# Linear-attention and FFN block on one core: another path and another order for the first chunk

## The reference

```python
xn = layernorm(x)                       # x: (8, 1024, 256), fp32
q, k, v = xn @ Wq.T, xn @ Wk.T, xn @ Wv.T          # 16 heads of 16
q, k = elu(q) + 1, elu(k) + 1
kv_state = sum over tokens of k (outer) v ; k_state = sum over tokens of k
attn = (q @ kv_state) / max(q . k_state, 1e-6)
local = conv over tokens, 3 taps per channel, of xn, + conv_b
attn_part = (attn + local) @ Wp.T + bp
ffn_part  = (silu(xn @ Wg.T) * (xn @ Wu.T)) @ Wd.T  # int weights / 127, hidden 768
out = x + attn_part + ffn_part
```

## Time and profile before

| | us |
|---|---|
| three runs, median | 522.21 (521.63 to 524.03) |
| the profiled execution | 524.11 |
| its span (first to last instruction) | 522.5 |
| PE busy | 499.1 (96%) |
| DVE busy | 436.5 (84%) |
| ACT busy | 332.8 (64%) |
| POOL busy | 129.7 (25%) |
| `project_kv(0)` of chunk (0, 1) starts | 48.10 |

### The profile page before, as it was taken

How to read it: one execution, slowest core, us unless ns; L and a number is a source line. 1 busy time by engine, 2 the same in 40 slices (tenths; PEclk the granted TensorE clock), 3 DMA queues, 4 the chain that set the end, 5 groups by cost and what they waited for, 6 DMA issues and landing times.

```text
span 522.5 us, 11639 instructions
## 1 busy us (share of the span) xinstructions
PE 499.1 (96%) x4249; PEld 303.9 (58%) x4249; DVE 436.5 (84%) x868; ACT 332.8 (64%) x521; POOL 129.7 (25%) x146
## 2 busy tenths in 40 slices
PE   7878999999999999999999999999999999999876
PEld 7435455665647566564756556475655647565465
DVE  4989798878888898888888888888888888886784
ACT  1576767667485766748576674857667485766730
POOL 3151414140321414032141403114140411400020
...
GB/s 231 274 57 111 87 69 94 42 130 39 157 41 110 94 41 127 42 153 40 113 88 41 126 44 150 40 115 86 40 129 43 149 40 120 43 54 31 1 41 80
DMA packets 70718, 45.90 MB, mean 88 GB/s; under 512 B 35488, under 2 KB 70176, under 8 KB 70688
## 3 DMA queue, kind: packets, MB, share of 16 engines
...
...
## 4 chain that ended last, share of the span: by engine, by line
PE 71%; DVE 11%; issue 7%; ACT 6%; DMA 2%; POOL 1%; SPq 1%; DVEq 0%; ACTq 0%
PE ps L970 16%; PE ps L1124 15%; PE ps L1054 15%; PE ps L1105 10%; PE ps L1114 10%; PE ps L1008 5%; ACT q_neg L477 3%; DVE hid L840 3%; DVE y L751 3%; DVE q_sb L809 2%; DMA wd_int<-in_L_ffn_w_down_dram 1%; DMA x_in<-in_L_attn_x_dram 1%; ACT act_g L486 1%; DVE hl L846 1%; DVE bn_raw L543 1%
## 5 line engine op out<-in xcount | busy, mean ns | idle before, releaser
L486 ACT ACTIVATE act_g<-ps,scales 128x512 f32<-128x512 f32 x96 | 65.9, 687 | 46.4 <-PE ps L1114 44.9
L840 DVE SCALAR_TENSOR_TENSOR hid<-act_g,scales,ps 128x512 f32<-128x512 f32 x96 | 71.4, 744 | 27.7 <-ACT act_g L486 27.6
L846 DVE TENSOR_TENSOR hl<-hid,hh 128x512 f16<-128x512 f32 x96 | 65.9, 687 | 1.5
L345 POOL TENSOR_TENSOR xT<-xh,xl 128x1024 f32<-128x1024 f16 x16 | 33.9, 2121 | 123.9 <-DMA xl<-xn_l 111.2
L1105 PE MATMUL ps<-xh,g_wh 128*128 128x512 f16 x192 | 57.6, 381 | 6.5 <-DVE hid L840 6.1
L494 ACT ACTIVATE hh<-hid 128x512 f16<-128x512 f32 x96 | 59.7, 622 | 5.3 <-DVE hid L840 5.3
L453 ACT ACTIVATE k_neg<-ps,scales 128x512 f32<-128x512 f32 x32 | 22.0, 687 | 57.7 <-PE ps L1054 57.7
L1114 PE MATMUL ps<-xl,u_wh 128*128 128x512 f16 x192 | 57.1, 379 | 0.0
L1114 PE MATMUL ps<-xl,g_wh 128*128 128x512 f16 x192 | 57.1, 379 | 0.0
L1105 PE MATMUL ps<-xh,u_wh 128*128 128x512 f16 x192 | 57.1, 379 | 0.0
L427 ACT ACTIVATE local<-xT,cb,cw 128x512 f32<-128x512 f32 x32 | 24.4, 806 | 42.7 <-POOL xT L345 39.3
...
## 6 DMA issues: line engine op xcount, KB each, us to landing
...
wg_int<-in_L_ffn_w_gate_dram SPq DMA_DIRECT2D x1, 768.0 KB, 7.3
wu_int<-in_L_ffn_w_up_dram SPq DMA_DIRECT2D x1, 768.0 KB, 8.8
wd_int<-in_L_ffn_w_down_dram SPq DMA_DIRECT2D x1, 768.0 KB, 6.0
wk_raw<-in_L_attn_Wk_dram ACTq DMA_DIRECT2D x1, 256.0 KB, 4.7
```

The source lines that it names most:

```text
L486: nc.scalar.activation(act_g[:, j % 2, :], ps[:, gate_bank(j), :], ACT.Silu, scale=silu_in).then_inc(silu_ready, 1)
L840: nc.vector.scalar_tensor_tensor(out=hid[:, j % 2, :], in0=act_g[:, j % 2, :], scalar=h_mul, in1=ps[:, gate_bank(j) + 1, :], op0=ALU.mult, ...
L846: nc.vector.tensor_tensor(hl[:, j, :], hid[:, j % 2, :], hh[:, j, :], ALU.subtract).then_inc(hl_ready, 1)
```

## The change

Only chunk (0, 0) is worked in another way; all later chunks keep their instructions, save that `x_high` and `x_low` of chunk (0, 1)'s step stand one j earlier (`FIRST_X_SPLIT` 2 for 3).

- x's first chunk is loaded in two halves, one from SP's queue and one from ACT's ahead of Wk and Wv. The second chunk of x comes right behind Wg and Wu, Wd comes ahead of Wp, and the bias last. The first chunk's two DMA transposes go.
- DVE normalises tiles 0 and 1, POOL tiles 2 and 3. PE transposes the eight 128x128 blocks of fp32 `xn` (`turn_first`), ACT copies them to `xT`, then makes `xh` from it, and POOL the rest `xl`.
- Keys and values are 16 fp32 matmuls of raw weights and `xT` (`project_first`), no split weights are needed for them; the scales of `key_parts` change to match. The split key and value weights are made later, for chunk (0, 1).
- POOL adds `k_sb`. `u_wh` moves from ACT to DVE.
- q is projected into banks 4 and 5 behind the keys and values, and read (`query_parts`, `relu_q`, `put_q`) after the FFN of the chunk.
- The maxima make four groups for three, and they pass PE between the new matmuls; `accumulate` goes behind `gate_up(0)`. The last group's scales and `attention_scales` come after `put_res`.
- PE's warm-up is 18 matmuls in one piece, for 24 and 16.

The core of the diff:

```diff
-        GROUPS = [["k", "v", "q"], ["g", "u"], ["d", "cw", "cb", "p"]]
+        GROUPS = [["k", "v", "q"], ["g", "u"], ["d"], ["cw", "cb", "p"]]
...
                      lambda channels: channels[:, c, :, :, :])
-            sp.dma_start(x_in[:, 0, :, :], x_v[0]).then_inc(x_loaded[0], 16)
+            sp.dma_start(x_in[:, 0, 0:2, :], x_v[0][:, 0:2, :]).then_inc(first_x[0], 16)
             load_weights("q", wqT, w_raw["q"][:, :, :])
             load_weights("g", wgT, ffn_rows("g", wgT))
             load_weights("u", wuT, ffn_rows("u", wuT))
-            sp.dma_start(bp_sb[:, :], bp.rearrange("(o n) -> o n", o=1).broadcast_to([P, D])).then_inc(bias_in, 16)
-            turn_x(0, 0)
+            sp.dma_start(x_in[:, 1, :, :], x_v[1]).then_inc(x_loaded[1], 16)
+            load_weights("d", wdT, ffn_rows("d", wdT))
             load_weights("p", wpT, w_raw["p"][:, :, :])
-            load_weights("d", wdT, ffn_rows("d", wdT))
             sp.dma_start(cw_raw[:, :, :], conv_w.rearrange("(k p) t -> p k t", p=P)).then_inc(small_in, 16)
             sp.dma_start(cb_raw[:, :], conv_b.rearrange("(k p) -> p k", p=P),
                          allow_slow_non_contiguous=True).then_inc(small_in, 16)
-            sp.dma_start(x_in[:, 1, :, :], x_v[1]).then_inc(x_loaded[1], 16)
+            sp.dma_start(bp_sb[:, :], bp.rearrange("(o n) -> o n", o=1).broadcast_to([P, D])).then_inc(bias_in, 16)
...
             nc.gpsimd.tensor_tensor(rstd[:, 0, :], var_eps[:, 0, :], half[:, :], ALU.pow).then_inc(rstd_ready, 1)
             pool.wait_ge(rstd_ready, 1)
-            normalise(0, 0)
-            normalise(0, 1).then_inc(xn_ready, 1)
-            normalise(0, 2)
+            normalise(0, 2).then_inc(xn_ready, 1)
             normalise(0, 3).then_inc(xn_ready, 1)
-            put_xT(0, 0)
-            add_x(0, 0)
+            pool.wait_ge(first_xh, 1)
+            nc.gpsimd.tensor_tensor(xl[:, 0, :, :, :], xT[:, 0, :, 1:1 + CHUNK].rearrange("p k (i t) -> p i k t", i=TILES),
+                                    xh[:, 0, :, :, :], ALU.subtract).then_inc(first_xl, 1)
+            for p in range(2):
+                pool.wait_ge(k_parts, p + 1)
+                nc.gpsimd.tensor_tensor(k_sb[:, 2 * p:2 * p + 2, :], k_exp[:, p, :, :], k_relu[:, p, :, :],
+                                        ALU.add).then_inc(k_ready, 1)
             def step(b, c, attend, ahead):
                 if ahead:
                     nb, ncx = (b, 1) if c == 0 else (b + 1, 0)
                     layernorm(nb, ncx)
+                    if isinstance(b, int) and b == 0 and c == 0:
+                        for p in range(2):
+                            pool.wait_ge(xn_h_ready, p + 1)
+                            tiles = slice(2 * p, 2 * p + 2)
+                            nc.gpsimd.tensor_tensor(xn_l[:, tiles, :], xn[:, tiles, :], xn_h[:, tiles, :],
+                                                    ALU.subtract).then_inc(xn_l_ready, 1)
+                        add_x(0, 0)
                     add_x(nb, ncx)
-                if ahead:
                     put_xT(nb, ncx)
...
+                        act.wait_ge(xh_turned, at(b, c, 16, -16))
...
-            x_high(0, 0)
-            high(kv_w[0][:, :, 0:D], w_raw["k"][:, :, :], "k", k_hi)
-            high(q_w[0][:, :, :], w_raw["q"][:, :, :], "q", q_hi)
+            for p in range(2):
+                act.wait_ge(first_turned, p + 1)
+                nc.scalar.activation(xT[:, 0, :, 1 + p * PAIR:1 + (p + 1) * PAIR], halves(FIRST_TURNED[p]),
+                                     ACT.Copy).then_inc(first_xT, 1)
+            act.wait_ge(first_xT, 2)
+            nc.scalar.activation(xh[:, 0, :, :, :], xT[:, 0, :, 1:1 + CHUNK].rearrange("p k (i t) -> p i k t", i=TILES),
+                                 ACT.Copy).then_inc(first_xh, 1)
             def middle_tap(b, c, k):
...
                     nc.scalar.activation(k_neg[:, p, :, :], ps[:, bank:bank + 2, 0:D], ACT.Relu,
-                                         scale=k_flip).then_inc(k_flipped, 1)
+                                         scale=k_flip if past else -1.0 / X_UP).then_inc(k_flipped, 1)
                     nc.scalar.activation(k_relu[:, p, :, :], ps[:, bank:bank + 2, 0:D], ACT.Relu,
-                                         scale=k_down)
+                                         scale=k_down if past else 1.0 / X_UP)
+                    if not past and p == 0:
+                        high(q_w[0][:, :, :], w_raw["q"][:, :, :], "q", q_hi)
...
-                if not past:
-                    high(u_w[0][:, :, :], ffn_raw["u"][:, :].rearrange("p (k n) -> p k n", k=KT), "u", gate_up_hi)
-                query_parts()
+                if past:
+                    query_parts()
+                else:
...
+                        high(kv_w[0][:, :, D:2 * D], w_raw["v"][:, :, :], "v", v_hi)
                     if j == D_SPLIT and not past:
...
                 return nc.vector.tensor_scalar(down, col(power, n), 1.0 / (X_UP * W_UP), None, ALU.mult)
             stats(0, 0)
-            for n in ("k", "v", "q"):
-                weight_maximum(n)
+            weight_maximum("k")
+            dve.wait_ge(rstd_ready, 1)
+            for i in range(2):
+                ins = nc.vector.tensor_scalar(xn[:, i, :], x_in[:, 0, i, :], neg_mean[:, 0, i:i + 1],
+                                              rstd[:, 0, i:i + 1], ALU.add, ALU.mult)
+            ins.then_inc(first_normed, 1)
+            weight_maximum("v")
+            weight_maximum("q")
+            weight_maximum("g")
             across(0)
-            x_low(0, 0, 0)
-            x_low(0, 0, 1)
+            weight_maximum("u")
             powers(0)
             feature_scales("q", q_flip, q_down)
             feature_scales("k", k_flip, k_down).then_inc(scaled[0], 1)
-            nc.vector.tensor_scalar(kv_w[0][:, :, D:2 * D], w_raw["v"][:, :, :], col(scale_up, "v"), None,
-                                    ALU.mult).then_inc(v_hi, 1)
-            low(kv_w[1][:, :, D:2 * D], w_raw["v"][:, :, :], "v", kv_w[0][:, :, D:2 * D], v_hi, 1, kv_lo)
-            low(kv_w[1][:, :, 0:D], w_raw["k"][:, :, :], "k", kv_w[0][:, :, 0:D], k_hi, 1, kv_lo)
...
-                if past:
-                    tap(pb, pc, 0, 0)
-                    tap(pb, pc, 1, 0)
-                if past and ahead:
+                if not past:
+                    gate_up_scales()
+                    gate_up_high("g", g_w)
+                    gate_up_high("u", u_w)
+                    stats(nb, ncx)
+                    gate_up_low_halves()
+                    hidden(0)
+                    weight_maximum("d")
+                    hidden(1)
+                    hidden_low(0)
+                    across(2)
+                    put_state()
+                    hidden(2)
+                    hidden_low(1)
+                    hidden(3)
+                    down_scales()
+                    hidden_low(2)
+                    hidden(4)
+                    hidden_low(3)
+                    hidden(5)
+                    hidden_low(4)
+                    hidden_low(5)
+                    down_low_half()
+                    late_maxima()
+                    low(kv_w[1][:, :, 0:D], w_raw["k"][:, :, :], "k", kv_w[0][:, :, 0:D], k_hi, 1, kv_lo)
+                    low(kv_w[1][:, :, D:2 * D], w_raw["v"][:, :, :], "v", kv_w[0][:, :, D:2 * D], v_hi, 1, kv_lo)
+                    across(3)
+                    put_res(0, DOWN)
+                    put_res(1, DOWN)
+                    attention_scales()
+                    relu_q()
+                    put_q()
...
+            def turn_first(p):
+                if p == 0:
+                    pe.wait_ge(first_normed, 1)
+                else:
+                    pe.wait_ge(xn_ready, 2)
+                for i in range(2):
+                    for k in range(KT):
+                        ins = nc.tensor.transpose(ps[:, FIRST_TURNED[p], k * PAIR + i * P:k * PAIR + (i + 1) * P],
+                                                  xn[:, 2 * p + i, k * P:(k + 1) * P], ident[:, :])
+                ins.then_inc(first_turned, 1)
+            def project_first(p, i):
+                pe.wait_ge(first_xT, p + 1)
+                t = 2 * p + i
+                for half, n in enumerate(("k", "v")):
+                    pe.wait_ge(w_in[n], 16)
+                    for k in range(KT):
+                        ins = nc.tensor.matmul(ps[:, t, half * D:(half + 1) * D], xT[:, 0, k, 1 + t * P:1 + (t + 1) * P],
+                                               w_raw[n][:, k, :], start=(k == 0), stop=(k == KT - 1))
+                if i == 1:
+                    ins.then_inc(kv_done, 1)
...
+                if not past:
+                    project_first(0, 0)
+                    turn_maxima(0)
+                    project_first(0, 1)
+                    spread_maxima(0)
+                    project_first(1, 0)
+                    turn_maxima(1)
+                    project_first(1, 1)
```

(18 more changed lines are left out.)

161 lines of the change are left out of this document (83 added, 78 removed).

## The result

The changed kernel took 528.38 us (median of 4 runs, 526.73 to 529.45), the kernel before 523.12 (4 runs) beside it: ratio 1.0102, 95% interval 1.0076 to 1.0129. It is slower by 5 to 6 us. A few executions far above the rest (here one of the kernel before, 1036.35, and later one of `keys_first`, 579.2) are left out of the ratios; the other three of the kernel before have a median of 522.21. The prediction said 520.4, between 517.2 and 523.4, and gave 0.10 to slower. The profiled execution of the changed kernel took 526.73, with a span of 525.1 and a mean granted clock of 0.993; the other three had 0.990.

The account below looks back on a forecast made before the run. PE, busy 96% of the span, was taken as the bound. Leads of 4.4 us at `gate_up(0)` and 4.2 at the next keys shrink to 1.8 at `gate_up(2)`, kept to the end: median 522.2 becomes 520.4, range 517.2 to 523.4.

Parts of the forecast that it names:

- Head, 4.4 earlier: From the start to the first `gate_up(0)`: it starts at 23.5 instead of 27.90, 4.4 us earlier (range 2.6 to 5.6).
- the locks beside POOL's two `k_sb`: In the head, DVE and POOL may shut each other out: up to 1.3 us, taken at 0.5.
- Lead at the keys of (0, 1), 4.2: Keys of chunk (0, 1) start at 43.9 instead of 48.10, 4.2 us earlier (1 to 6).
- The 20.4 from `gate_up(0)` to the keys: First chunk: 17.4 us of PE's work, 2.3 of waits and 0.7 for a lock; before, 20.2.
- Given back in the second chunk: Keys of (0, 1) to its `gate_up(2)`: 15.4 us for 13.0, so `gate_up(2)` comes at 59.3, 1.8 earlier.
- The sum of DVE's row: Second chunk: DVE's work ending with `put_k(1)`, for which `accumulate(1)` waits, 11.5 us with the 0.4 before it.
- ACT's part: Second chunk: ACT no later than DVE, its `silu(0)` 12.9 us after the keys' start, when `gate_up(0)` is done.
- x_high and x_low one j earlier, 0: Chunk (0, 1): PE waits for `hid(3)` instead of `hid(4)`, `hid(5)` comes as before: cost 0.
- The clock: Rival: the head's 16 fp32 matmuls fall to half pace after the warm-up, 7.2 us more, 527.6; chance 0.08.

Follow-up runs that it names:

- keys_first: `x_later` plus, in the second chunk, keys and q ahead of work that can wait on ACT and DVE: 521.76 us, ratio 0.9986 to the kernel before.
- all_fillers: Changed kernel with identity matmuls in PE's gaps in the head, second chunk and near the end, no work moved: 523.41 us, ratio 1.0017 to the kernel before.
- unchanged: Changed kernel without any edit, run again on the same chip as `all_fillers`: 527.58 us, ratio 1.0106 to the kernel before.
- u_on_act: Changed kernel with `u_wh` made by ACT behind its last `k_exp` instead of by DVE: 524.92 us, ratio 1.0053 to the kernel before.
- filler: Changed kernel with thirteen identity matmuls in PE's gaps of the second chunk, all waits kept: 525.12 us, ratio 1.0046 to the kernel before.
- x_later: Changed kernel with `x_high` and `x_low` of chunk (0, 1) back behind j = 3: 524.0 us, ratio 1.0040 to the kernel before.
- head_filler: Changed kernel with eight identity matmuls on PE between q's projection and the wait for `u_wh`: 524.69 us, ratio 1.0057 to the kernel before.
- xT_waits: Changed kernel with POOL's `xT` for chunk (1, 0) waiting for DVE's last `hl`: 524.87 us, ratio 1.0052 to the kernel before.

## Why the prediction was wrong

- **Head, 4.4 earlier**: 3.5. x landed sooner (4.31 for 5.6), so the first fp32 matmul came 1.0 earlier than forecast. The fp32 matmuls kept whole pace; with the maxima between them they took 8.9 for 8.4, and that is the 0.49 of PE's wait behind the lock of `spread` beside POOL's `xl`; the prediction had `xl` hidden by PE's work and put no lock there. The larger error is the locks beside POOL's two `k_sb`, priced at 0.5: 0.42 at `power` and 1.01 at `u_wh`. `u_wh` has one tensor input and is stopped as one with two is. In this, 2.02 for 1.01, the trace agrees with the rule of the Trainium skill ("SBUF — State Buffer", Who interferes with whom), the rule that I gave less weight than its absence from the rows.
- **Lead at the keys of (0, 1), 4.2**: 3.1, that is the head's error and 0.2 more. The 20.4 from `gate_up(0)` to the keys was 20.60.
- **Given back in the second chunk**: 15.4 from the keys to `gate_up(2)`; measured 17.29. Without the half pace (1.63) it is 15.66. The sum of DVE's row was right, and so was ACT's part.
- **x_high and x_low one j earlier, 0**: this step failed. It cost 1.5. I looked only at which `hid` PE would wait for, and not at who is released: x turned earlier lets POOL's `xT` start earlier, among the last `hl`. It is the collision of the earlier trace rows at 44.80, in a new place.
- **The clock**: this step failed too, and it is the largest error, 4 of the 7.3 us between a forecast of 1.8 faster and a loss of 5.5. It did not turn the sign alone: with the clock held the kernel is still 1.3 to 1.7 slower, by the locks in the head and the place of x. I had the half pace as a rival, but put it at the fp32 matmuls, behind a gap of about two microseconds after the warm-up, and asked only there. There PE was idle for 0.35 and 0.25 only, besides the transposes. The long gaps were those that the prediction itself had worked out elsewhere: its numbers gave PE 1.3 us to wait ahead of `gate_up(0)` (q's end at 22.2, then 23.5) and 2.8 in the second chunk (11.9 for a stretch of work that took PE 9.1 in the kernel before, 48.10 to 57.23), each entered at its own length and with nothing behind it. Behind them stand the stretches of the head and of the second chunk, 1.6 each where they occur; with the one near the end the half pace makes 4.2 us (`all_fillers` against `unchanged`). The trace of the kernel before held such a fall, 0.63 in 508:512 behind the wait of 2.10, and it makes most of the 1.9 by which the profiled execution lay above the median; the prediction says that no row shows one. The Trainium skill ("TensorE: Matmul & The Clock Gate", What's actually happening) says that the clock falls after an idle stretch; the fillers bear it out.

The sum in the terms of the runs: 0.5 gained up to `gate_up(2)` (61.12 to 60.6 at whole pace), 1.5 lost to the place of x, which makes 1.0 where the medians of the runs at full clock say 1.3 to 1.7; the half pace adds 4, in part at the end's old wait.

What stays open: why the same gaps are followed by half pace in one execution and not in another (`u_on_act`, and 25 of 61 executions of the kernel before), why the wait of 2.10 near the end is followed by it in all three profiles of the changed kernel and in none of `filler`, `x_later`, `head_filler` and `xT_waits`, which don't touch it, and the few tenths between the two reckonings of the waits. The Trainium skill (same page and section) says that the clock's window runs free of the kernel, so that the place of a change differs between executions; that would fit the first point, but no run here tests it.
